# Handing four of 25 subtractions per chunk from GpSimd to VectorE in a graph attention layer

## What is computed

```
q, k, v = (x @ wq + bq), (x @ wk + bk), (x @ wv + bv)      # n x 2 heads x 64
alpha = einsum('ehc,ehc->eh', q[dst], k[src]) / sqrt(64)
amax  = segment_max(alpha, dst)
ex    = exp(alpha - amax[dst])
denom = segment_sum(ex, dst)
out   = segment_sum(ex / (denom[dst] + 1e-16) * v[src], dst).mean(over heads) + x @ ws + bs
```

## Time and profile before

| what | value |
|---|---|
| median of 3 runs | 3559.18 us (3556.36 to 3571.11) |
| the profiled execution's own time | 3564.24 us |
| its span in the trace | 3562.4 us |
| VectorE busy, of the span | 2896.8 us, 81% |
| GpSimd busy, of the span | 2663.7 us, 75% |
| TensorE busy, of the span | 3187.2 us, 89% |
| ScalarE busy, of the span | 999.1 us, 28% |

### The profile page before, as it was taken

The page is one execution under the profiler, slowest core; times in us unless marked ns, Lnnn a source line. Parts: engine busy times, 40 slices in busy tenths (PEclk is TensorE's granted clock), DMA queues, the critical chain, the costliest instruction groups (busy, mean ns, idle before and its releaser), DMA issues.

```text
span 3562.4 us, 64347 instructions
## 1 busy us (share of the span) xinstructions
PE 3187.2 (89%) x20040; PEld 1823.5 (51%) x20040; DVE 2896.8 (81%) x8886; ACT 999.1 (28%) x1689; POOL 2663.7 (75%) x1764
## 2 busy tenths in 40 slices
PE   4899999999999999999999999976788888899996
PEld 3566666666666666666666666642222222322222
DVE  6688888888888888888888888868677775877886
ACT  3111111111111111111111111133455554233433
POOL 2288888888888888888888888861787888476874
PEclk7999999999999999999999999987899999999998
DMA  8633333333333333333333333315545452232320
GB/s 311 247 49 50 45 44 50 50 50 49 50 44 45 49 50 50 49 50 46 44 49 50 50 49 50 39 2 151 151 127 150 129 151 75 78 89 76 89 64 9
DMA packets 265753, 271.38 MB, mean 76 GB/s; under 512 B 145252, under 2 KB 224717, under 8 KB 265673
## 3 DMA queue, kind: packets, MB, share of 16 engines
q1 hardware_dynamic: 90905, 163.09, 15.3%
q0 software_dynamic: 131712, 19.76, 12.7%
q10 hardware_dynamic: 43056, 87.49, 8.0%
HBM read 189.11 MB, written 81.07 MB: 76 GB/s over the span
## 4 chain that ended last, share of the span: by engine, by line
POOL 47%; PE 19%; issue 17%; DVE 6%; DMA 5%; ACT 3%; SPq 3%; POOLq 1%; DVEq 0%
POOL edge_counts L486 27%; POOL nodes_and_gaps L477 14%; PE PS L1404 6%; PE PS L1427 6%; DMA edge_counts<-small 4%; POOL scores L541 4%; PE PS L1436 3%; SPq L366 2%; POOL counts_and_logs L524 1%; DVE scores L1142 1%; DVE PS L1153 1%; DVE counts_and_logs L1128 1%; PE PS L1416 1%; DMA edge_counts<-counts_and_logs 1%; ACT scores L729 1%
## 5 line engine op out<-in xcount | busy, mean ns | idle before, releaser
L1303 PE MATMUL PS<-scores 128*128 128x320 bf16 x11760 | 1707.2, 303 | 132.5 <-DVE scores L974 69.1
L1303 PEld LDWEIGHTS PS<-scores 128*128 128x128 bf16 x11760 | 1156.9, 99 | 664.4 <-DVE scores L974 160.5
L486 POOL DMA_INDIRECT edge_counts<-small x752 | 1211.6, 1611 | 282.0 <-issue 282.0
L541 POOL TENSOR_TENSOR scores<-scores,max_of_targets 125x896 f32<-125x896 f32 x335 | 701.5, 2140 | 191.4 <-ACT max_of_targets L724 142.0
L477 POOL DMA_INDIRECT nodes_and_gaps<-xj_rows,small x588 | 580.9, 988 | 242.4 <-issue 162.8
L974 DVE TENSOR_SCALAR scores<-scores,small 128x192 bf16<-128x192 bf16 x3136 | 748.2, 304 | 3.5
L889 DVE SCALAR_TENSOR_TENSOR scores<-scores,small,PS 128x512 bf16<-128x512 f32 x784 | 573.0, 731 | 0.0
L1142 DVE TENSOR_TENSOR scores<-PS,counts_and_logs 125x896 f32<-125x896 f32 x350 | 377.8, 1082 | 204.0 <-PE PS L1404 76.9
L624 ACT ACTIVATE scores<-nodes_and_gaps 128x512 bf16<-128x512 f32 x98 | 61.7, 630 | 1403.6 <-DVE nodes_and_gaps L952 929.8
L729 ACT ACTIVATE scores<-scores 125x896 f32<-125x896 f32 x350 | 329.9, 948 | 372.8 <-POOL scores L541 365.9
L1404 PE MATMUL PS<-q_features,k_features 64*125 64x448 f32 x1400 | 371.1, 612 | 68.0 <-DVE scores L1142 65.1
(11 more groups left out here) (192 smaller groups left out, 2124.0 us busy)
## 6 DMA issues: line engine op xcount, KB each, us to landing
counts_and_logs<-edge_counts SPq DMA_DIRECT2D x70, 980.0 KB
scores<-tile_keys ACTq DMA_DIRECT2D x96, 512.0 KB
edge_counts<-counts_and_logs SPq DMA_DIRECT2D x50, 766.0 KB
edge_counts<-counts_and_logs SPq DMA_DIRECT2D x35, 980.0 KB
running_max<-fetch_targets ACTq DMA_DIRECT2D x48, 312.5 KB
max_of_targets<-fetch_targets ACTq DMA_DIRECT2D x48, 312.5 KB
edge_counts<-small POOLq DMA_INDIRECT x752
nodes_and_gaps<-xj_rows,small POOLq DMA_INDIRECT x588
```

The lines of the kernel that those rows point to most:

```text
L486: pool.indirect_dma_start(cnt_dram, bass.IndirectOffsetOnAxis(ap=index[:, s:s + 1], axis=0), value[:, s:s + 1], None, compute_op=ALU.add). ...
L541: nc.gpsimd.tensor_tensor(t, t, MB, ALU.subtract).then_inc(sem("shifted"), 1)
L1303: ins = nc.tensor.matmul(PS[:, b, 0:HI * F], onehot[:, s, b * P:b * P + 128], spread[:, s, i].rearrange("p h f -> p (h f)"), start=first a ...
```

## The change

`by_vector` is true for tiles 8, 12, 18 and 22 of chunks 0 to 5 as well. GpSimd's loop skips these tiles, VectorE's loop over the following chunk gets a `shift` behind `score` and `running` of tiles 8, 12, 18 and 22, and ScalarE waits for the other semaphore before these four exponentials. Chunk 6, the second attention layer and all that comes before stay as they are.

```
+BY_VECTOR = (8, 12, 18, 22)
...
         def by_vector(g, i):
 
-            return g == LAST and i % QN in (1, 3, 4)
+            return i % QN in (1, 3, 4) if g == LAST else g < CH - 1 and i in BY_VECTOR
```

## The result

The changed kernel takes 3598.2 us (median of 4 runs, 3593.8 to 3599.0), the kernel before 3560.3 us beside it: ratio 1.0099, 95% interval 1.0075 to 1.0123. It is slower by 38 us. The forecast was 3580 us, 21 more than before, in a range of 3564 to 3598; the measured time stands at the range's upper edge.

The account below looks back on a forecast made before the run. GpSimd looked like the bound, but its waits ended with VectorE. Five periods at 2.4 us (12.0), the first 0.8 and two misses 8.8 made 21.6 us, giving 3580 us; range 3564 to 3598.

Parts of the forecast that it names:

- What bounds the kernel: Six chunk periods of the first attention layer: GpSimd looks like the bound, but each of its three waits ends with VectorE.
- the last rival: GpSimd paces the chunk, so the moved shifts save 4.2 us per chunk, 25 us in six: 3534 us; chance 0.06.
- The cost of the port: A moved tile takes 2.06 us from GpSimd; VectorE pays 1.02 to 1.02 + 4.4 us, by what GpSimd is doing.
- A to B: Stretch from the end of a chunk's first `steepen` to its second's: 1.9 us longer, 0.3 in the first period.
- the sums of tile 9: TensorE's weighted sums, between the two `steepen`: ready about 18.3 us after the first, before score 11 is reached at 19.1.
- B to the maximum: Stretch from the second `steepen`'s end to the next maximum: 0.5 us longer, or 4.9 where shift 22 misses its place.
- Eight instructions later, at 20.9, comes shift 22: VectorE reaches shift 22 20.9 us after the second `steepen`, getting in before the third `take_gap`; score 23 0.5 us later.
- The price of a miss: Shift 22 falling behind the third `take_gap`: score 23 4.9 us later, 4.4 more than in the good case.
- late arrivals: VectorE reaching shift 18 over 10.65 us after the second `steepen`, finding GpSimd in tile 19; two counted, 8.8 us.
- the second rival: Tile 22 misses its place in nearly every chunk with a third `take_gap`: 33 us, 3592 us; chance 0.17.
- the gapless run: VectorE has no gap from score 10 to the second `steepen`, so shift 12 adds its whole 1.0 us.

Follow-up runs that it names:

- Experiment 9: Kernel before the change, with GpSimd no longer waiting for `steepen` before its tiles 5 and 15: 3668.0 us, ratio 1.0279.
- Experiment 3: Only tile 8 goes to VectorE, against the kernel before the change: ratio 1.0037.
- Experiment 1: Changed kernel with ScalarE's `next_h` moved from behind the exponential of tile 18 to behind that of tile 17: 3584.9 us, ratio 1.0083 to the kernel before.
- 4: Only tile 12 goes to VectorE, against the kernel before the change: ratio 1.0044.
- 8: Kernel before the change, no tile moved, VectorE's two reciprocals put ahead of tiles 3 and 7: 3567.8 us, ratio 1.0003.
- 7: Kernel before the change, with only tile 7 moved to VectorE and the two reciprocals put ahead of tiles 3 and 7: 3576.4 us, ratio 1.0044.
- 11: Kernel before, with only tile 7 on VectorE, its shift behind score 5, and reciprocals ahead of tiles 3 and 7: 3547.3 us, ratio 0.9957.
- experiment 10: Kernel before, GpSimd not waiting for `steepen` before tiles 5 and 15, reciprocals ahead of tiles 3 and 7: median 3608.3 us; ratio 1.0044 from four shortest runs.

## Why the prediction was right and wrong

**What bounds the kernel** was right: GpSimd's waits were tied to VectorE's chain, and taking 24 tiles off GpSimd made it wait longer. Experiment 9 shows how tied: without the wait the time is 108 us worse. So the last rival, the faster one, did not come.

**The cost of the port** was right. Shift 8 was issued at A + 9.2 and ended at 13.7, score 10 started at 15.6 (forecast 15.7), shift 12 lasted 1.1 us without waiting. A shift issued in `take_gap` waits for its end, as read from the earlier trace rows.

**A to B** was forecast 1.9 us longer (0.3 in the first period), 9.8 in all; it was 19.8. The step that failed is the term "the sums of tile 9 ... ready at about 18.3, before score 11 is reached at 19.1", with the clock kept outside the sum as "up to 0.9 us". TensorE's clock fell behind the wait for tile 8 in all six periods, the sums were ready at A + 20.0 in period 2 and later in others, and score 11 started at 20.1 to 21.6. This came to about 1.0 to 2.3 us per period, and to some 3 in the first, where the same delay hit a chain with no reciprocals. Experiment 3 separates it from the port: 0.7 us where the clock stayed full behind the wait, 1.9 to 2.8 where it did not.

**B to the maximum** was forecast 0.5 us longer in four periods and 4.9 in two, 11.8 in all; it was 16.4. The step that failed is "Eight instructions later, at 20.9, comes shift 22": score 21 was not reached at 17.0, since exponential 18, `next_h` and the scores of tile 20 hang on shift 18. I had followed the exponentials to the weighted sums, but not to what else stands in ScalarE's queue behind exponential 18. So shift 22 missed in all four periods that have both `next_h` and a third `take_gap`; the first, which has no `next_h`, and the sixth, which has no third `take_gap`, came out at 33.7 and 34.3. The price of a miss was right, 38.1 against 33.7 us. Two of the four, periods 4 and 5, are the late arrivals that the forecast had counted (shift 18 at B + 10.62 and 10.73); 2 and 3 are the ones it had not. Experiment 1 takes `next_h` away from there, and four misses become one.

The result is the second rival's, "missed in nearly every chunk that has one", which had 0.17 and 3592 us. That its 33 us came so near the 36.3 is partly luck: its A to B was 10 us too small, as the forecast's, and its B to the maximum, 23 us, too large against 16.4. In period 1 that stretch even became 1.5 us shorter: a low stretch of TensorE's clock that stood at B + 28.9 to 32.3 there before the change was gone after it. The port, the gapless run and the late arrivals of the forecast are all there; it had too little for the clock behind tile 8, and it had no path from shift 18 over `next_h` to shift 22.

**Where a gain went.** In 4 and 8 part of the change shows up in B to the maximum, which reads either near 33.6 or near 35.2. In the kernel before, two of six periods have the longer one. The window at the turning of the maximum in period 3 and in period 4 of the kernel before:

```profile
2734.00:2738.00 4.00, 3.70 (x14) 1.89 (x16) 1.62 (x3) 0.00 (x0) 1.87 (x1) 0.57 1.05 286
2814.00:2818.00 4.00, 3.96 (x27) 2.36 (x27) 1.37 (x2) 1.07 (x2) 1.63 (x1) 1.00 1.06 289
```

The granted clock is 0.57 in the one and 1.00 in the other. The same holds in the traces of experiments 3, 4, 7, 8 and 11: where B to the maximum is 35.0 to 35.2 us a low stretch begins between B + 27.8 and B + 29.5, and where it is 33.4 to 33.6 none does. What decides where the low stretch falls in a period is open; I made no run for it.

## What to carry to other kernels

Where two engines share a port and one holds it for a whole instruction, the cost of moving work is set by what the other engine is doing when the moved instruction is issued: look for the long instructions near the new place, and put it early in a run of short ones, not next to the boundary. Follow each delayed result through every queue that waits for it, also to the unrelated instruction behind it. And a wait that looks like lost time can be what keeps a resource free; try it alone before counting it as a gain.

## What I had not expected of the hardware

The port is not shared fairly in every case. VectorE's shifts got it at the next boundary of GpSimd's instructions, with 1.1 to 5.1 us each; but in experiment 9 the second `steepen` of period 1 stayed shut out while GpSimd went from one instruction to the next 11 times, 30.6 us in all. The first `steepen` of the same period, issued 0.6 us before a boundary, took 3.0 us. The time of issue alone does not settle it: both that long `steepen` and the second one of period 1 in experiment 10 were issued 1.2 us before the end of a GpSimd tile, and the latter got in at that boundary and took 3.6 us. Why the one is let in and the other is not stays open. The Trainium skill ("SBUF — State Buffer", section "🔬 SBUF: two separate sides") says that whoever starts first has the shared pair for the whole instruction; the trace agrees for the single instruction, and what happens between two of them no run here settles.
